# A transformer block on one core: queries kept whole in SBUF and their rests made by GpSimd, the last key tile folded by VectorE

## What is computed

```python
DIM, HEADS, DHEAD, CTX_DIM = (256, 16, 64, 192)
def _attn(x, ctx, Wq, Wk, Wv, Wo, bo):
    q = (x @ Wq).reshape(b, n, HEADS, DHEAD)
    k = (ctx @ Wk).reshape(b, m, HEADS, DHEAD)
    v = (ctx @ Wv).reshape(b, m, HEADS, DHEAD)
    sim = jnp.einsum('bihd,bjhd->bhij', q, k) * DHEAD ** (-0.5)
    attn = jax.nn.softmax(sim, axis=-1)
    out = jnp.einsum('bhij,bjhd->bihd', attn, v).reshape(b, n, INNER)
    return out @ Wo + bo
h = _ln(x, g1, be1)
x = _attn(h, h, Wq1, Wk1, Wv1, Wo1, bo1) + x
h = _ln(x, g2, be2)
x = _attn(h, context, Wq2, Wk2, Wv2, Wo2, bo2) + x
h = _ln(x, g3, be3)
y = h @ Wp + bp
a, gate = (y[..., :FF_HID], y[..., FF_HID:])
x = a * jax.nn.gelu(gate, approximate=False) @ W2 + b2 + x
```

## Time and profile before

| | us |
|---|---|
| Runs | 1985.23, 1987.01, 1987.35; median 1987.01 |
| The profiled execution, its time | 1986.85 |
| Its span, first to last instruction | 1985.1 |
| PE busy in the span | 1971.6 (99%) |
| DVE, ACT, POOL busy | 1393.6 (70%), 1150.6 (58%), 1444.1 (73%) |
| Granted TensorE clock, mean | 1.000 |

### The profile page before, as it was taken

How to read it: one execution, slowest core, us unless ns; L and a number is a source line. 1 busy time by engine, 2 the same in 40 slices (tenths; PEclk the granted TensorE clock), 3 DMA queues, 4 the chain that set the end, 5 groups by cost and what they waited for, 6 DMA issues and landing times.

```text
span 1985.1 us, 32079 instructions
## 1 busy us (share of the span) xinstructions
PE 1971.6 (99%) x12056; PEld 1345.1 (68%) x12056; DVE 1393.6 (70%) x2382; ACT 1150.6 (58%) x2042; POOL 1444.1 (73%) x752
## 2 busy tenths in 40 slices
PE   9999999999999999999999999999999999999999
PEld 7555655667565556755655666565569999888888
DVE  6688687666768786587687666767867888744443
ACT  6665576565556665465666555656756766533332
POOL 3699899978979997899799798979896665200000
PEclk9999999999999999999999999999999999999999
DMA  7301000011000000020000001010030420000100
GB/s 256 138 38 64 17 22 22 12 33 54 22 12 12 33 12 33 1 75 11 11 12 22 33 12 54 22 33 1 22 106 22 150 65 1 1 22 33 33 11 32
DMA packets 40506, 77.63 MB, mean 39 GB/s; under 512 B 5920, under 2 KB 29600, under 8 KB 38304
## 3 DMA queue, kind: packets, MB, share of 16 engines
q1 hardware_dynamic: 40352, 75.59, 11.5%
HBM read 51.46 MB, written 24.12 MB: 38 GB/s over the span
## 4 chain that ended last, share of the span: by engine, by line
PE 92%; DVE 3%; POOL 3%; issue 1%; ACT 1%; POOLq 0%; DVEq 0%
PE score L577 21%; PE score L556 18%; PE score L703 9%; PE attn_project L512 8%; PE attn_project L688 5%; PE attn_project L717 5%; PE score L524 5%; PE score L658 4%; PE score L626 3%; PE attn_project L538 3%; PE first_score L538 3%; PE score L562 3%; POOL acc L1528 2%; PE first_score L672 1%; PE first_score L588 1%
## 5 line engine op out<-in xcount | busy, mean ns | idle before, releaser
L1528 POOL TENSOR_TENSOR acc<-acc,pT 128x1024 f32<-128x1024 f32 x384 | 916.7, 2387 | 54.4 <-POOL acc L1528 0.9
L1271 ACT ACTIVATE pT<-score 128x1024 f32<-128x1024 f32 x512 | 515.7, 1026 | 89.1 <-PE score L562 53.5
L556 PE MATMUL score<-qk 64*128 64x512 f32 x3072 | 467.5, 405 | 2.5 <-DVE hT L852 1.9
L577 PE MATMUL score<-pT,vT 128*64 128x512 f32 x1952 | 432.3, 595 | 0.0
L556 PEld LDWEIGHTS score<-qk 64*128 64x128 f32 x3072 | 267.2, 184 | 97.0 <-ACT pT L1271 20.9
L907 DVE TENSOR_REDUCE nmax<-first_score 128x2 f32<-128x1024 f32 x256 | 311.0, 1215 | 2.4 <-PE first_score L538 2.4
L907 DVE TENSOR_REDUCE nmax<-attn_project 128x2 f32<-128x1024 f32 x256 | 311.0, 1215 | 1.0 <-PE attn_project L538 0.9
L577 PEld LDWEIGHTS score<-pT,vT 128*64 128x64 f32 x1952 | 134.7, 137 | 259.5 <-issue 252.6
L1525 POOL TENSOR_TENSOR acc<-pT 128x1024 f32<-128x1024 f32 x64 | 153.4, 2396 | 68.6 <-ACT pT L1271 68.6
L512 PE MATMUL attn_project<-hT,wqk 128*128 128x512 f32 x738 | 186.3, 401 | 0.0
L703 PE MATMUL score<-hT,wp 128*128 128x512 f32 x768 | 183.7, 395 | 0.0
(11 more groups left out here) (201 smaller groups left out, 3007.2 us busy)
## 6 DMA issues: line engine op xcount, KB each, us to landing
wqk<-wqk_parts SPq DMA_DIRECT2D x24, 512.0 KB, 3.3
xres<-x_middle SPq DMA_DIRECT2D x10, 512.0 KB, 3.7
raw_v<-in_L_xattn_Wv SPq DMA_DIRECT2D x8, 512.0 KB, 4.9
keys_all<-keys SPq DMA_DIRECT2D x1, 4096.0 KB, 13.1
values_all<-values SPq DMA_DIRECT2D x1, 4096.0 KB, 13.2
wqk_parts<-wqk SPq DMA_DIRECT2D x8, 512.0 KB, 3.3
out_x<-xres SPq DMA_DIRECT2D x7, 512.0 KB, 3.0
xres<-in_x SPq DMA_DIRECT2D x3, 1024.0 KB, 5.7
```

Of the source, the lines that this page charges most:

```text
L556: last = e.matmul(bank, key_part(P, h, r, jt), queries1[P % 2][r, w, c * BANK:(c + 1) * BANK], start=(fresh and part == 0), stop=(not fres ...
L577: last = e.matmul(banks[bank][head * DH:(head + 1) * DH, :], vT[:, v_slot(D, jt), c0:c0 + DH], pT[:, jt, head, :], start=(jt == 0), stop=( ...
L1271: e.activation(pT[:, jt].rearrange("p h n -> p (h n)"), SC[R % 2][:, :], ACT.Exp).then_inc(s.exponential, 1)
L1528: e.tensor_tensor(total, total, pT[:, jt], ALU.add).then_inc(s.probs_added, 1)
```

## The change

It has two halves.

**Queries.** ScalarE's copy out of PSUM (scaled by 1/8) now goes unrounded to SBUF, into the place where the rest will be (`queries_whole`, the same bytes as the lo part), and this copy alone frees bank PJ. One step later ScalarE rounds it from SBUF (`round_queries`, between `make_shift` and `write_oT`), and GpSimd subtracts in place at the end of its step (`split_queries`, after the additions). L897 is gone from VectorE, but for the three query halves that are made ahead of the loop (`FIRST_QUERIES`). The unrounded copy of the first half of the keys, formerly in a tile of its own (`keys_full`), moves into the place of the keys' rest.

**Sums.** GpSimd adds the tiles 0 to 6 only (`ADDS` = 6 additions a step). VectorE folds tile 7 by itself (`fold_last`, right after it has turned the maxima, ahead of `split_wo1` and `fold_sums`), into a place of its own in `folded`. `sum_quads` multiplies both, 64 columns where there were 32, and VectorE adds the two halves in one small reduction (`totals`) before it inverts. The last exponential of a step waits until the last tile of the step before is folded (`last_folded`).

```diff
@@ -138,7 +139,12 @@
             ("wo1", [PAIRS, DIM], F32R))
+        _, qk1_whole, _, qk0_whole = overlay(
+            ("before_qk", [PRING * N + 3 * TILES * BANK + (2 * ARING + 1) * BANK], F32), ("qk1_whole", [4 * N + BANK], F32),
+            ("sums_between", [2 * BANK], F32), ("qk0_whole", [4 * N + BANK], F32))
         PAIR = BANK // 2
+        queries_whole = [tile[:, N:2 * N] for tile in (qk0_whole, qk1_whole)]
+        keys_whole = [tile[:, 2 * N:3 * N].rearrange("p (c n) -> p c n", c=CHUNKS) for tile in (qk0_whole, qk1_whole)]
         queries1 = [tile[:, 0:2 * N].rearrange("p (w n) -> p w n", w=2) for tile in (qk0, qk1)]
@@ -285,6 +291,14 @@
         keys_of = numbered((P, u) for P in range(B * PAIRS) for u in range(CHUNKS))
+        queries_of = numbered((P, u) for P in range(B * PAIRS) for u in range(2, 2 + CHUNKS))
+        FIRST_QUERIES = [(0, 2), (0, 3), (1, 2)]
+
+        def queries_rest(unit):
+
+            if unit in FIRST_QUERIES:
+                return s.first_queries_lo, queries_of[unit]
+            return s.queries_lo, queries_of[unit] - len(FIRST_QUERIES)
@@ -357,6 +371,11 @@
             return jobs + [("out1", *tile, through[i % len(through)]) for i, tile in enumerate(out1_tiles(C))]
+
+        def queries_unit(C):
+
+            P, c = divmod(C, CHUNKS)
+            return [(P + 1 + c, 3 - c)] if C >= 0 and P + 1 + c < B * PAIRS else []
@@ -513,7 +532,8 @@
                 last.then_inc(s.qk_projected, 1)
-                free[bank] = ((s.split_lo, qk_of[P, u]),)
+                free[bank] = ((s.split_lo, keys_of[P, u]) if u < 2 else queries_rest((P, u)) if (P, u) in FIRST_QUERIES
+                              else (s.queries_kept, queries_of[P, u] - len(FIRST_QUERIES)),)
@@ -547,9 +567,10 @@
                 if part < len(TERMS):
-                    for u in (2 + c, jt // TPC):
-                        need.wait_ge(s.split_hi, qk_of[P, u])
-                        need.wait_ge(s.split_lo, qk_of[P, u])
+                    need.wait_ge(s.queries_hi, queries_of[P, 2 + c])
+                    need.wait_ge(*queries_rest((P, 2 + c)))
+                    need.wait_ge(s.split_hi, keys_of[P, jt // TPC])
+                    need.wait_ge(s.split_lo, keys_of[P, jt // TPC])
                     if part == 0:
@@ -583,11 +604,12 @@
                 need.wait_ge(s.acc_folded, C + 1)
+                need.wait_ge(s.last_folded, C + 1)
                 need.wait_ge(s.quads_made, 4)
                 bank_free(bank)
-                e.matmul(banks[bank][:, 0:2 * QB], quads[:, :], folded[:, :], start=True, stop=True
-                         ).then_inc(s.summed, 1)
-                free[bank] = ((s.sum_inverted, C + 1),)
+                both = folded[:, 0:2] if C % 2 == 0 else folded[:, 0:3:2]
+                e.matmul(banks[bank][:, 0:4 * QB], quads[:, :], both, start=True, stop=True).then_inc(s.summed, 1)
+                free[bank] = ((s.sum_totalled, C + 1),)
@@ -884,21 +906,21 @@
                                 keys_hi[P % 2][:, u, PAIR:2 * PAIR].bitcast(F32), ALU.subtract)
-                e.tensor_tensor(later, later, keys_full[:, :], ALU.subtract).then_inc(s.keys_changed, 1)
+                e.tensor_tensor(later, later, keys_whole[P % 2][:, u, PAIR:], ALU.subtract).then_inc(s.keys_changed, 1)
                 need.wait_ge(s.keys_changed, n)
-                need.wait_ge(s.split_hi, qk_of[P, u])
+                need.wait_ge(s.split_hi, n)
                 e.tensor_tensor(keys_lo[P % 2][:, u, PAIR:], later, keys_hi[P % 2][:, u, 0:PAIR].bitcast(F32),
-            def split_queries(P, u, bank):
+            def split_first_queries(P, u, bank):
                 span = slice((u - 2) * BANK, (u - 1) * BANK)
-                need.wait_ge(s.split_hi, qk_of[P, u])
+                need.wait_ge(s.queries_hi, queries_of[P, u])
                 hi, lo = (queries1[P % 2][:, w, span] for w in range(2))
                 e.scalar_tensor_tensor(lo, banks[bank], SCALE, hi.bitcast(F32), ALU.mult, ALU.subtract
-                                       ).then_inc(s.split_lo, 1)
+                                       ).then_inc(s.first_queries_lo, 1)
             def split_qk(P, u, bank="PJ"):
-                (change_keys if u < 2 else split_queries)(P, u, bank)
+                (change_keys if u < 2 else split_first_queries)(P, u, bank)
@@ -924,19 +946,29 @@
+            def fold_last(C):
+
+                need.wait_ge(s.exponential, TILES * (C + 1))
+                need.wait_ge(s.summed, C - 1 if C > 1 else 0)
+                e.tensor_reduce(folded[:, 1 + C % 2], pT[:, TILES - 1].rearrange("p h (b n) -> p (h b) n", n=SQUARE), AX.X,
+                                ALU.add, apply_transpose=True).then_inc(s.last_folded, 1)
+
             def fold_sums(C):
-                need.wait_ge(s.probs_added, (TILES - 1) * (C + 1))
+                need.wait_ge(s.probs_added, ADDS * (C + 1))
                 need.wait_ge(s.summed, C)
-                e.tensor_reduce(folded[:, :], acc[:, C % ARING].rearrange("p h (b n) -> p (h b) n", n=SQUARE), AX.X, ALU.add,
+                e.tensor_reduce(folded[:, 0], acc[:, C % ARING].rearrange("p h (b n) -> p (h b) n", n=SQUARE), AX.X, ALU.add,
                                 apply_transpose=True).then_inc(s.acc_folded, 1)
                 need.wait_ge(s.summed, C + 1)
+                e.tensor_reduce(totals[:, :], banks[bank][:, 0:4 * QB].rearrange("p (w q) -> p q w", w=2), AX.X, ALU.add
+                                ).then_inc(s.sum_totalled, 1)
+                need.wait_ge(s.sum_totalled, C + 1)
                 for head in range(2):
                     r = slice(head * DH, (head + 1) * DH)
-                    last = e.reciprocal(rsum[r, :], banks[bank][r, head * QB:(head + 1) * QB])
+                    last = e.reciprocal(rsum[r, :], totals[r, head * QB:(head + 1) * QB])
                 last.then_inc(s.sum_inverted, 1)
@@ -959,8 +991,8 @@
                 for job in jobs:
-                    if job[0] == "qk":
-                        split_qk(*job[1:])
+                    if job[0] == "qk" and job[2] < 2:
+                        change_keys(*job[1:])
                     elif job[0] == "sum":
@@ -1071,6 +1103,8 @@
                     turn_max(C + 1)
+                if C + 1 < NC:
+                    fold_last(C)
                 if C == NC - 1:
@@ -1243,14 +1278,24 @@
                 if u >= 2:
-                    e.activation(queries1[P % 2][:, 0, (u - 2) * BANK:(u - 1) * BANK], banks[bank], ACT.Copy, scale=SCALE
-                                 ).then_inc(s.split_hi, 1)
+                    span = slice((u - 2) * BANK, (u - 1) * BANK)
+                    if (P, u) in FIRST_QUERIES:
+                        e.activation(queries1[P % 2][:, 0, span], banks[bank], ACT.Copy, scale=SCALE
+                                     ).then_inc(s.queries_hi, 1)
+                    else:
+                        e.activation(queries_whole[P % 2][:, span], banks[bank], ACT.Copy, scale=SCALE
+                                     ).then_inc(s.queries_kept, 1)
                     return
                 need.wait_ge(s.keys_changed, keys_of[P, u] - 1)
-                e.copy(keys_full[:, :], banks[bank][:, 0:PAIR]).then_inc(s.keys_copied, 1)
+                e.copy(keys_whole[P % 2][:, u, PAIR:], banks[bank][:, 0:PAIR]).then_inc(s.keys_copied, 1)
                 e.copy(keys_hi[P % 2][:, u, PAIR:], banks[bank]).then_inc(s.keys_rounded, 1)
                 e.copy(keys_hi[P % 2][:, u, 0:PAIR], banks[bank][:, PAIR:]).then_inc(s.split_hi, 1)
+
+            def round_queries(P, u):
+                span = slice((u - 2) * BANK, (u - 1) * BANK)
+                need.wait_ge(s.queries_kept, queries_of[P, u] - len(FIRST_QUERIES))
+                e.copy(queries1[P % 2][:, 0, span], queries_whole[P % 2][:, span]).then_inc(s.queries_hi, 1)
@@ -1267,7 +1312,9 @@
                     need.wait_ge(s.attended, R - TILES + 1)
-                    need.wait_ge(s.probs_added, (TILES - 1) * (R // TILES - 1) + max(jt, 1))
+                    need.wait_ge(s.probs_added, ADDS * (R // TILES - 1) + min(max(jt, 1), ADDS))
+                    if jt == TILES - 1:
+                        need.wait_ge(s.last_folded, R // TILES)
                 e.activation(pT[:, jt].rearrange("p h n -> p (h n)"), SC[R % 2][:, :], ACT.Exp
@@ -1435,6 +1482,8 @@
                     make_shift(C + 1)
+                for unit in queries_unit(C - 1):
+                    round_queries(*unit)
                 write_oT(C)
@@ -1515,6 +1564,12 @@
+            def split_queries(P, u):
+                span = slice((u - 2) * BANK, (u - 1) * BANK)
+                need.wait_ge(s.queries_hi, queries_of[P, u])
+                e.tensor_tensor(queries1[P % 2][:, 1, span], queries_whole[P % 2][:, span],
+                                queries1[P % 2][:, 0, span].bitcast(F32), ALU.subtract).then_inc(s.queries_lo, 1)
+
             def add_probs(R):
@@ -1632,7 +1687,8 @@
                 for jt in range(1, TILES):
```

(5 more changed lines are left out.)

27 lines of the change are left out of this document (15 added, 12 removed).

## The result

The changed kernel takes 1970.09 us (median of 4 runs, 1969.88 to 1970.6), the kernel before 1986.41 us (4 runs, 1985.23 to 1987.35). The ratio is 0.9918, 95% interval 0.9906 to 0.993: 16.3 us less, where 7.2 less were forecast, and outside the range. The profiled spans are 1985.1 us before and 1968.2 after.

What follows compares the result with a forecast made beforehand. The prediction took TensorE as the bound, with VectorE's row maxima and ScalarE's exponentials nearly as long in the score phase. Terms -8.4 - 0.6 - 0.4 + 2.6 - 0.6 + 0.2 = -7.2 us gave 1979.7 us, range 1975.0 to 1986.7.

Steps and rivals of the forecast that it cites:

- Ordinary steps, -8.4: 44 loop steps without L897 on VectorE: first row maximum earlier, 0.19 us saved each, -8.4 us in all.
- Rival 1: VectorE alone holds the score phase, so each ordinary step gains 0.34 us: 1973.1 us; chance 0.08.
- rival 2: Something else takes L897's place and ordinary steps gain nothing: 1988.6 us, no change; chance 0.16.
- the prediction's last sentence on step 19: In the score phase, the rest of the gain is lost to ScalarE's back-to-back exponentials: 0.34 us earlier saves 0.19.
- Steps behind a norm, -0.6: Six steps where a norm's work precedes the keys on VectorE: 0.1 us gained in each, -0.6 us.
- step 61, -0.4: A step behind a norm where `attend` waits for a late row maximum: 0.35 us counts in full, -0.4 us.
- Steps 1 to 4, +2.6: First steps, where the split of Wo1 leaves no cover for `fold_last`: 0.65 us lost in each, +2.6 us.
- Step 63, +0.2: Last step, where the fold is waited for and comes behind `totals`: +0.2 us.
- The tail, -0.6: After the last step: GpSimd's last addition ends earlier, VectorE has `fold_last` in its place, -0.6 us.
- rival 3: `fold_last` held up beside GpSimd's additions makes `sum_quads` 1.0 us late in some 60 steps: about 2040 us; chance 0.06.
- The rule against it: Avoid `tensor_reduce` on hot paths; with VectorE's total as the bound, the change would be 48 us slower.

Runs made afterwards that it cites:

- e1: The kernel before, with the unrounded keys' copy moved and a filler added, so large tiles except `hT` lie 640 bytes lower; 1978.81 us, ratio 0.9964.
- e9: The kernel before, with only the declaration of one small tile (`sd`, 128 bytes per partition) moved ahead of `hT`; 1979.2 us, ratio 0.9961.
- e2: The changed kernel plus a filler of 640 bytes a partition, giving the large tiles their old addresses; 1978.45 us, ratio 0.9968 against the kernel before.
- e4: The changed kernel at the old addresses, with VectorE still making the queries' rests out of PSUM (sums' half alone); 1989.7 us, ratio 1.0021 against the kernel before.
- e5: The changed kernel with `fold_last` placed behind `fold_sums` of the step before; 1967.18 us, ratio 0.9902 against the kernel before.
- e12: The queries' half alone at the changed kernel's addresses, `split_queries` on VectorE behind `fold_sums`; 1974.92 us, ratio 0.9938 against the kernel before.
- e3: The changed kernel at the old addresses with the queries' half alone: GpSimd keeps 7 additions, no `fold_last`; 1996.94 us, ratio 1.0057 against the kernel before.

## Why the prediction was wrong

**The step that failed** is one that the prediction never wrote down: it took the length of every matmul that the change doesn't touch as given. It costed what the diff does to instructions, and not what it does to addresses. The removed `keys_full`, the wider `folded` and the new `totals` brought `hT` and the weights from 128 to 0 bytes past a multiple of 256, and 1890 matmuls that read both (768 + 384 + 738), and the 384 cross scores, run 1 to 2% faster. e1 and e9 show this alone (ratios 0.9964 and 0.9961), e2 shows the rest without it (0.9968). By the medians the addresses are worth 6.9 us in the kernel before (e1) and 8.4 us in the changed one (1978.45 less 1970.09, not run side by side). The rates times the counts give 3.3 + 1.9 + 2.5 + 0.9 = 8.6 us, but the 2.5 of `project_qk` come through only in part: in steps 5 to 62 the changed kernel is 3.3 us faster than e2, and e1 2.2 us faster than the kernel before. In their place the loop starts at another moment, which alters how long the split of Wo1 takes (e1). The 7.2 us of the change itself and e1's 6.9 make 14.1 of the 16.3 us measured; the 2.2 us left are less than the spread of the kernel before alone (1984.14 to 1987.79) and are given to nothing.

At equal addresses the forecast of -7.2 us met the median of e2 (1978.45 for 1985.68; by the ratio's interval 4.0 to 8.7 us less). That it met to the digit is luck: the loop gave less than forecast, step 63 and the tail gave more, and the first steps are unsteady. Term by term:

- *Ordinary steps, -8.4.* Right in kind: first maximum at 1.57 us, `attend` at 9.09 us in odd steps. In even steps it starts at 9.15, where step 18 of the kernel before, even and covered like step 19, had 9.08; why is open. e2 has periods of 19.38 and 19.31 for 19.50: 0.15 a step on the mean, not 0.19, so -6.8 for the -8.4. Rival 1 and rival 2 both fell: the waits went over to ScalarE, as the prediction's last sentence on step 19 had it. In the changed kernel steps 5 to 62 give more, -11.2 for e2's -7.9: of these 3.3 us 2.2 lie in the seven steps with a value projection, and the rest fits the faster `project_qk`.
- *Steps behind a norm, -0.6; step 61, -0.4.* Steps 13 and 14 took 21.17 and 20.31 us in e2 for 21.33 and 20.54, so 0.16 and 0.23 for the 0.1 taken. `attend` of step 61 came 0.3 us earlier.
- *Steps 1 to 4, +2.6.* Unsteady, as named, and the size a guess: +1.2 in the changed kernel, +4.4 in e4, +4.5 in the profiled execution of e2 beside the 1.7 us that the lower clock cost there. The clock is a term that the prediction didn't have. What decides is the split of Wo1 (L950, now L982): 2.66 and 2.63 us in steps 1 and 2 of the changed kernel, which took 20.92 and 20.93 us for 19.92 and 20.03; then 0.65 us in step 3, which took 19.26. In e2 all four took 2.62 to 2.85 us, and steps 3 and 4 are 3.3 us longer than in the changed kernel, the lower clock aside. Without both, e2's profiled 1982.38 us would be about 1977.4, an estimate; its four shorter runs took 1977.74 to 1978.86, but none of them has a trace. The prediction put 0.65 us on each of four steps; it is 1 us or more, or a gain of 0.7.
- *Step 63, +0.2.* The wrong sign: -1.0. It saw that the fold waits for GpSimd there (1.2 us) and gave that as `totals`' cost alone. GpSimd's missing addition ends that wait whole: `attend` 8.64 us after the scores for 9.65. Where GpSimd has one addition less (e2, e4, e5) it is 8.61 to 8.62, where it has all seven (e1, e9, e12) 9.64 to 10.49.
- *The tail, -0.6.* Right in kind, -0.9: the wait for scaled probabilities went from 1.1 to 0.2 us.
- *`totals`* took 0.23 us for the 0.25 taken; the wider `sum_quads` 0.43 us for 0.41. *`fold_last`* took 1.25 us, and rival 3 did not come.

**What the prediction did not see at all** is that the halves need each other. It costed GpSimd's exchange at nothing in the loop, which is right for the whole change. e3 shows that the subtraction alone makes GpSimd the bound (+11 us), and e4 that the folding alone costs 4 us and gives nothing in ordinary steps. The statement that no matmul in the loop waits for GpSimd held for the earlier trace rows only because 7 additions and a scaling fit into a step with about 0.6 us to spare (7 x 2.39, 6 gaps of 0.14 and 1.30 make 18.9 of 19.5 us).

**The rule against it** (the Trainium skill, "VectorE: DVE Perf Modes", "Rules for kernel authors", on `tensor_reduce`) does not decide here, as weighed: VectorE is busy for 44 us more, and the time fell.
